# A fused two-layer program: routing and token transfers first at its head, another order of the feed-forward, scalings and last groups at its end

## The reference, cut to what matters

```python
# x: (8, 512, 128), two layers
xn = layernorm(x)
x = x + mamba(xn) + moe(xn)          # layer 0
xn = layernorm(x)
x = x + window_attention(xn) + swiglu(xn)   # layer 1
# mamba: proj = xn @ in_proj.T; conv over 4 steps, silu -> u; x_proj, three rmsnorms -> dt, B, C
#   h = exp(dt*A) * h + (dt*u) * B   (512 steps, 256 channels, 16 states);  y = sum(h * C) + u * D
#   out = (y * silu(gate)) @ out_proj.T
# moe: top_idx = argmax(xn @ gate_w.T + gate_b + expert_bias)  (8 experts)
#   out = w2[e] @ relu(w1[e] @ xn + b1[e]) + b2[e] for the token's expert e
# window_attention: 16 heads of 8, keys at most 32 positions away, softmax, then @ Wo + bo
# swiglu: (silu(xn @ wg.T) * (xn @ wu.T)) @ wd.T, hidden width 384, weights given as int32 / 127
```

## Time and profile before

| | us |
|---|---|
| median of 3 runs | 1018.65 (1018.41 to 1019.23) |
| the profiled execution | 1021.74 |
| its span | 1019.9 |
| busy: TensorE, VectorE, ScalarE, GpSimd | 810.4, 760.9, 638.1, 434.0 |

### The profile page before, as it was taken

How to read it: one execution, slowest core, us unless ns; L and a number is a source line. 1 busy time by engine, 2 the same in 40 slices (tenths; PEclk the granted TensorE clock), 3 DMA queues, 4 the chain that set the end, 5 groups by cost and what they waited for, 6 DMA issues and landing times.

```text
span 1019.9 us, 15614 instructions
## 1 busy us (share of the span) xinstructions
PE 810.4 (79%) x5226; PEld 560.0 (55%) x5226; DVE 760.9 (75%) x1059; ACT 638.1 (63%) x1976; POOL 434.0 (43%) x248
## 2 busy tenths in 40 slices
PE   1855788776788788988898799889888986899785
PEld 0622787664554565556555656565556554556443
DVE  7769443445867897789778977897888888786475
ACT  0233566644579566956795689568956884595554
POOL 2368331104564156516742573266426632571100
PEclk9957899998789888999999989999999998899898
DMA  6564799775434254235414541464145414550000
GB/s 218 172 193 137 233 280 299 225 203 132 119 79 98 60 143 99 64 103 145 115 46 120 149 99 41 119 152 106 32 123 148 106 41 124 129 122 15 19 11 12
DMA packets 85952, 123.20 MB, mean 121 GB/s; under 512 B 8560, under 2 KB 43760, under 8 KB 85744
## 3 DMA queue, kind: packets, MB, share of 16 engines
q1 hardware_dynamic: 79584, 115.38, 41.6%
q0 software_dynamic: 6288, 6.82, 3.0%
HBM read 106.21 MB, written 12.29 MB: 116 GB/s over the span
## 4 chain that ended last, share of the span: by engine, by line
PE 36%; DVE 24%; ACT 14%; issue 12%; POOL 8%; DMA 3%; SPq 1%; DVEq 0%; POOLq 0%; ACTq 0%
DVE hst L818 9%; PE more L1446 6%; ACT pexp L1118 5%; PE y_bank L1314 5%; DVE dBu L810 5%; POOL xs_d L1184 3%; ACT dA L1040 3%; POOL hc L1216 3%; ACT pT L1131 2%; PE work L1333 1%; PE work_l L1458 1%; PE work L1359 1%; PE work L1496 1%; PE work_l L1428 1%; PE work L1292 1%
## 5 line engine op out<-in xcount | busy, mean ns | idle before, releaser
L1216 POOL TENSOR_TENSOR hc<-hst,bcr 128x1024 f32<-128x1024 f32 x116 | 273.7, 2360 | 423.1 <-DVE dBu L810 401.6
L818 DVE TENSOR_TENSOR_SCAN hst<-dA,dBu 128x1024 f32<-128x1024 f32 x128 | 291.8, 2280 | 1.9 <-ACT dA L1040 0.9
L1040 ACT ACTIVATE dA<-dt,neg_a 128x511 f32<-128x511 f32 x256 | 171.0, 726 | 34.0 <-DVE hst L818 31.4
L810 DVE TENSOR_TENSOR dBu<-dtu,bcr 128x1024 f32<-128x1024 f32 x128 | 160.4, 1253 | 11.9 <-DMA bcr<-bc_d 1.5
L1314 PE MATMUL y_bank<-pk,hc 128*128 128x128 f32 x1024 | 153.9, 299 | 14.5 <-POOL hc L1216 10.9
L1314 PEld LDWEIGHTS y_bank<-pk,hc 128*128 128x128 f32 x1024 | 128.8, 154 | 50.8 <-issue 23.3
L1446 PE MATMUL more<-pk,pexp 128*96 128x128 f32 x480 | 109.4, 301 | 48.5 <-ACT pexp L1118 43.0
L1446 PEld LDWEIGHTS more<-pk,pexp 128*96 128x96 f32 x480 | 58.1, 129 | 95.4 <-issue 51.9
L1118 ACT ACTIVATE pexp<-work,nmax 128x96 f32<-128x96 f32 x240 | 77.9, 337 | 30.8 <-DVE nmax L965 30.7
L1131 ACT COPY pT<-more 96x512 f32<-96x512 f32 x120 | 69.9, 582 | 36.8 <-PE more L1446 36.3
L965 DVE TENSOR_REDUCE nmax<-work 128x4 f32<-128x384 f32 x60 | 33.4, 557 | 78.3 <-PE work L1367 57.5
(11 more groups left out here) (363 smaller groups left out, 1524.7 us busy)
## 6 DMA issues: line engine op xcount, KB each, us to landing
bcr<-bc_d SPq DMA_DIRECT2D x128, 512.0 KB, 5.1
qbd<-in_wx SPq DMA_DIRECT2D x8, 578.0 KB, 4.6
o_all<-in_wx SPq DMA_DIRECT2D x8, 578.0 KB, 4.8
pT<-in_wx SPq DMA_DIRECT2D x8, 578.0 KB, 5.1
kT<-in_wx SPq DMA_DIRECT2D x8, 578.0 KB, 5.1
vw<-in_wx SPq DMA_DIRECT2D x8, 578.0 KB, 5.0
xs_d<-rbuf POOLq DMA_DIRECT2D x1, 2560.0 KB, 9.7
hst<-in_hidden SPq DMA_DIRECT2D x8, 256.0 KB, 6.6
```

The costliest lines, as they stand in the source:

```text
L810: v.tensor_tensor(dBu[:], dtu[par], bcr[n % RING][:, 0:1, :].to_broadcast([P, NH, L]), ALU.mult).then_inc(s_dBu, 1)
L818: v.tensor_tensor_scan(hst[n % 2][:].rearrange("p h t -> p (h t)"), dA[n % 2][:].rearrange("p h t -> p (h t)"), dBu[:].rearrange("p h t -> ...
L1040: s.activation(dA[n % 2][:, h, 1:L], dt[par][:, h, 1:L], ACT.Exp, scale=neg_a[:, h, n:n + 1]).then_inc(s_dA, 1)
L1216: g_.tensor_tensor(hc[n % 2][:], hst[n % 2][:], bcr[n % RING][:, 1:2, :].to_broadcast([P, NH, L]), ALU.mult).then_inc(s_hc, 1)
```

## The change

At the head, `LEAD` now holds the statistics, normalisation, transposes and gates of all eight sequences, then four constants, `pick`, `count`, `place`, the other constants, and the scatters of sequences 0 to 2. Each engine walks through `LEAD` before turn -1. The scatters of sequence 3 stand in slot 8 of turn -1, the others in slot 9. The four first loads of x go ahead of the packed weights, the feed-forward weights come later. The zeros are written from a zeroed half of `dA[1]` and issued ahead of the last power on GpSimd. The wait for all constants moves from the start of TensorE, ScalarE and GpSimd to the units that use them. The expert stage begins in slot 3.

At the end, the feed-forward of sequence 6 leaves turn 7 for `LAST`, behind `y_end`, with banks of its own (5 to 7, which the preparation and `dBu` no longer need). The scaling goes from VectorE to GpSimd. The feed-forward of sequence 7 comes in slots 2 to 7 with its two halves a slot apart, and writes to `z[0]` and `dA`. The averages of sequence 6 move from slot 3 to 7 and its output from 4 to 8 and 9. The last groups are written out by hand.

```diff
-MOE_AT = 4
+MOE_AT = 3
...
+FFN_UNITS = ("fg", "fs", "fu", "fh", "rden")
...
 def last_turn():
     a, f = B - 1, B - 2
-    out = [("y_end", 0, a), ("rdT", 0, f), ("gated", 0, a), ("yT", 0, a)]
-    out += [(name, 0, a) for name in ("out", "x1", "ln_a", "ln_b", "q", "k", "v0", "v1")]
-    for t in range(G + 3):
-        if 1 <= t <= G:
+    out = [("y_end", 0, a), ("fg", 0, f), ("fu", 0, f), ("gated", 0, a), ("fs", 0, f), ("fh", 0, f), ("yT", 0, a),
+           ("fg", 1, f), ("out", 0, a), ("fu", 1, f), ("x1", 0, a), ("ln_a", 0, a), ("fs", 1, f), ("fh", 1, f),
+           ("fg", 2, f), ("fu", 2, f), ("ln_b", 0, a), ("fs", 2, f), ("fh", 2, f), ("rden", 0, f), ("rdT", 0, f)]
+    out += [(name, 0, a) for name in ("q", "k", "v0", "v1")]
+    for t in range(G):
+        if t >= 1:
             out.append(("exp", t - 1, a))
...
+    out += [(name, k, a) for name, k in (
+        ("exp", G - 1), ("scale", G - 2), ("turn", G - 2), ("values", G - 3), ("proj", 2), ("own", G - 4),
+        ("scale", G - 1), ("turn", G - 1), ("own", G - 3), ("values", G - 2), ("y_last", 2), ("own", G - 2),
+        ("values", G - 1), ("own", G - 1), ("proj", 3), ("y_last", 3))]
...
-LEAD = [("stats", 0), ("stats", 1), ("norm", 0), ("stats", 2), ("norm", 1)]
+def lead():
+    out = [("stats", 0)]
+    for k in range(B):
+        if k + 1 < B:
+            out.append(("stats", k + 1))
+        out += [("norm", k), ("xT", k)]
+        if k > 0:
+            out.append(("gate", k - 1))
+    out += [("gate", B - 1), ("route_consts", 0), ("pick", 0), ("count", 0), ("place", 0), ("consts", 0)]
+    return out + [("scatter", k) for k in range(3)]
...
-    put(-1, 14, ("scatter", 0))
+    put(-1, 8, ("scatter", 3))
+    put(-1, 9, *[("scatter", k) for k in range(4, B)])
...
                     v.reciprocal(rden[:, :, k], den[:, :, k]).then_inc(s_rden, 1)
-                    dve.wait_ge(s_rden, b + k + 1)
-                    v.tensor_tensor(pexp[k % 2][:], pexp[k % 2][:], rden[:, :, k:k + 1].to_broadcast([P, RG, KW]),
-                                    ALU.mult).then_inc(s_norm, 1)
...
+                    elif name == "scale":
+                        pool.wait_ge(s_rden, b + k + 1)
+                        g_.tensor_tensor(pexp[k % 2][:], pexp[k % 2][:], rden[:, :, k:k + 1].to_broadcast([P, RG, KW]),
+                                         ALU.mult).then_inc(s_norm, 1)
```

More of the change, by code:

```diff
@@ L229, in l1_bank @@
         return LAST_BANK[key]
+    if b == B - 2 and key in FFN_BANK:
+        return FFN_BANK[key]
     return L1_BANK[key]
@@ L802, in early @@
                             v.tensor_tensor(bias_rest[:], bias_rest[:], bias_part[:], ALU.subtract).then_inc(s_bias, 1)
+            for name, k in LEAD:
+                early(name, k)
             def times_b(n, b, par):
@@ L1032, in early @@
                     last.then_inc(s_mr, 1)
+            for name, k in LEAD:
+                early(name, k)
             def decays(n, b, par):
+                if b == 0 and n == 0:
+                    act.wait_ge(s_const, CONSTS)
+                if b == 0 and n == 1:
+                    act.wait_ge(s_zero, 16)
                 if n == 0:
```

175 lines of the change are left out of this document (92 added, 83 removed).

## The result

| | before | changed |
|---|---|---|
| median of the runs | 1018.62 us (4 runs, 1018.41 to 1019.23) | 1028.13 us (4 runs, 1027.01 to 1032.25) |
| ratio, 95% interval | | 1.0081 [1.0051, 1.0111] |
| profiled execution, span | 1021.74 us, 1019.9 us | 1027.95 us, 1026.2 us |

The forecast was 1010.5 us, faster; by the medians the kernel got 9.5 us slower.

The account below looks back on a forecast made before the run. Limits seen: first expert tile waiting for scattered tokens, the expert-tile loop, then a chain to the first scores and VectorE in the score groups. Head +1, way to scores -7.4, loop 0, last groups -1.7: 1010.5 us, range 1004 to 1018.

Parts of the forecast that it names:

- Head, routing: Start of program: eight norms end near 24, routing takes 9.4 us, slot table at 35.5 instead of 55.58 us.
- Head, what waits for it: First sequence's preparation, moved behind routing: convolution at 41.8, first scan step at 84.1 instead of 74.66 us.
- Head, the expert stage: First expert tile at about 105.5, where it was 105.0; head +1 us, between -4 and +12.
- The scan's start holds it: First expert tile waits behind sequence 1's second convolution matmuls, 15.1 us after the first scan step; nothing left of 20 us.
- rival (3): Head gives back the end's gain: first scan step near 90, first tile near 112, +7.5; 1017 us, no change; chance 0.10.
- Middle: Sequences 1 to 6: no engine's order changes, so the stretch is carried over at its present time.
- End, the way to the first scores: Last scan to first scores: y_end 4.3 us earlier, projections at full clock; -7.4 us, bounds -4 and -8.
- End, the score loop: Sixteen score groups: 6.5 us round three groups, 2.15 per group against 2.23; net 0, from -2.5 to +5.
- The last groups: Last exponential to last y: 7.6 to 9.2 us where it was 9.9; -1.7, between 0 and -2.3.
- The sum: Whole kernel: +1 - 7.4 + 0 - 1.7 = -8.1 us, giving 1010.5 us for the median.
- late head: The case of rival (3): late first scan step and first tile, head +7.5 us; 1017 us; chance 0.10.
- slow loop: Score loop slower: GpSimd handovers 0.2 us each, averages stop two groups, +4; 1014.5 us; chance 0.12.

Follow-up runs that it names:

- e5: The changed kernel with 14 wide matmuls on zeros ahead of everything on TensorE: 1029.50 us, ratio 1.0114 to the kernel before.
- e9: The changed kernel with the expert stage two slots earlier (MOE_AT = 1 instead of 3): 1031.51 us, ratio 1.0107 to the kernel before.
- e13: e12 with VectorE's first instruction held until the tenth of 32 wide matmuls, a plain delay at the start: 1020.61 us, ratio 1.0016.
- e16: The kernel of e13 run and profiled once more, nothing changed: 1020.36 us in one run.
- e2: The kernel before with the changed tail alone, head of before: 1019.73 us, ratio 0.9997.
- e3: As e2, with the scaling of the last sequence's groups back on VectorE: 1015.74 us, ratio 0.9967 to the kernel before.
- e4: The kernel before with only y_end ahead of sequence 6's feed-forward; loop and last groups of before: 1017.97 us, ratio 0.9981.
- e7: e4 with sequence 6's final sums at group 10 and sequence 7's feed-forward at groups 4, 6, 8: 1012.30 us, ratio 0.9945.
- e10: e7 with each part of sequence 7's feed-forward split over two groups, parts two groups earlier: 1016.33 us, ratio 0.9970.
- e11: e7 with the change's order of the last groups: 1011.47 us, ratio 0.9918 to the kernel before.
- e12: e11 with 22 wide matmuls on zeros on TensorE at the start: 1010.98 us, ratio 0.9918 to the kernel before.
- e15: The changed kernel measured and profiled again, nothing changed: 1028.86 us against 1020.21 for the kernel before, ratio 1.0097.
- e6: The kernel before with only the last sequence's scalings moved to GpSimd: 1023.05 us against 1019.89, ratio 1.0030.
- e14: Changed head with preparation before routing and ten wide matmuls on zeros ahead, with e11's tail: 1018.80 us, ratio 0.9967 to the kernel before.

## Why the prediction was wrong

**Head, routing: the step that failed first.** "Eight of them in one piece ... end near 24" and the 9.4 us of routing were right (23.16 + 1.11; 32.66 to 42.09). Between the two the prediction has no term for TensorE at all: it lets the routing begin at 26 us, when VectorE is done, as if the transposes and gates ended with the norms. They end at 32.6, because TensorE does them at 2.45 us a sequence, no faster than the norms come, and only from 12.52 on. In the head of before the same work ran behind wide convolutions at 0.60 + 0.96 us, and hid beside other work; at the start of the program it runs at the lower level. Slot table: 35.5 forecast, 42.1 measured. e5 shows this cause by itself: with TensorE warm the slot table is there 5.0 us earlier.

**Head, what waits for it.** The order of the chain was right and so were most durations: from slot table to first convolution 6.3 forecast, 7.3 measured; from there to the first scan step 42.3 forecast, 43.1 measured. One link was wrong: the scatters ahead of xdn were to set the time of the transposes behind it, but xdn was done at 73.86 and the transposes at 75.53 waited for VectorE's sg (74.78 + 0.69). That they came 26.3 us behind the first convolution, 25.5 forecast, is luck in that link. All 8.2 us by which the first scan step missed 84.1 came down from the routing, but for 1.8. But the forecast itself already moved that step by 9.4 us, and the prediction let all of it vanish behind the expert stage's start.

**Head, the expert stage.** "The scan's start holds it" was right: the second convolution matmuls of sequence 1 start 15.1 us behind the first scan step, as forecast, and the first tile starts behind them (107.45 + 5.32), not behind the scatters, the last of which ended at 94.4. The allowance for a scan step inside the stage was fair (129.6 against 128.4 us, e9 shows where it ends to be fair). With the first tile at 115 instead of 105.5 the head's term became +8.9 instead of +1. This is the sum's largest error, 7.9 us; rival (3) had that path (a late first scan step takes the first tile with it), with +7.5, but from other causes (both convolutions at 6.31 us, slow scatters, late loads), and came to "no change" with an end of -9. The head's own range reached to +12, so the measured +8.9 lies inside it.

**Middle.** Taken at its present time; it lost 2.2 us in the means. The stretch takes 692.6 and 694.3 us in the changed kernel's two profiles and 689.3 to 695.1 in the eight with the head of before, so the loss is not clear of their spread. The two long turns of the changed kernel, 3.4 us together, are seen in both; no order changed there, and e13 and e16 exclude the mere shift, so their cause stays open.

**End, the way to the first scores.** Right in size and cause: -7.4 forecast, -7.6 measured; out projection 2.02 us, q and k 1.98, at full clock. With the head of before, q and k took 3.78 us in seven of nine profiles with this order (e2, e3, e4, e7, e10, e11, e16; 3.23 in e12, 1.98 in e13), and only 5.65 us were had, near the 5.8 that the prediction gave for a fallen clock. The full 7.6 of the changed kernel is thus in part luck. The Trainium skill (TensorE: Matmul & The Clock Gate, section HAM oscillation) has idle gaps bring the clock down and a filled stream keep it. The stream was not wholly filled here, and the rule does not tell the two cases apart: before q and k TensorE idled 1.25, 0.31 and 0.3 us in the changed kernel as in e4, which has the same order up to there, and q and k took 1.98 us at a granted clock of 1.00 in the one, 3.78 at 0.57 to 0.58 in the other.

**End, the score loop: the second step that failed.** Forecast 0, measured +5.5 us in the mean: +4.7 in e15 with TensorE at the full level, +6.3 in the first profile. The way round was counted as 6.5 us over three groups with feed-forward parts "about 2.2 us per part as before". It left out where the parts stand. TensorE's two matmuls (1.7 us) lie between a group's turn and the next scores, so on the way round; before, VectorE did the part's two products meanwhile, and in the change it has them one group later and idles. e10 measures this at 1.7 us of waiting over three parts, and as much again where TensorE's clock falls behind the longer idle time. The scaling on GpSimd took 0.83 us, less than the 1.01 forecast, and is the largest piece all the same: with it each of seven rounds of the changed order is 0.3 us longer in e15 than in e3, 2.2 us together. The remaining 0.7 us of the 4.7 lie between e3, without its stretch at the lower level, and e10, whose sums of sequence 6 stand two groups later. So the way round, with the parts on it, was longer than VectorE's work, and the 0.56 us freed there bought nothing. In the order of before (e6) the loop itself did not suffer from the scaling, as forecast, but from the averages ahead of it in GpSimd's queue; the prediction had that wait as a term, 1.2 us at group 7, and in the changed kernel it is nothing: the averages run from 980.70 to 983.63, in GpSimd's idle time before the scaling at 986.04. The Trainium skill's rule (GPSIMD Engine Reference, section Engine selection) pointed that way, by another price: it has two-input elementwise work about twice as slow on GpSimd, and 0.83 against 0.56 is 1.5 times.

**The last groups.** Forecast -1.7, measured -1.3 in the change, and -2.0 where the scaling is on VectorE (e11 against e7's and before's end).

**The sum.** +1 - 7.4 + 0 - 1.7 became +8.9 + 2.2 - 7.6 + 5.5 - 1.3 = +7.7. The head and the loop each came out inside or just at the end of the range that the prediction gave them (up to +12 and +5); the range of the whole, up to 1018, allowed only 7.5 us above the forecast and so left out that both go wrong. The chances have the same fault: head and loop were each given a chance of going wrong with the other right, and cases in which both do (late head 0.10, slow loop 0.12) had none of their own.

The version to take is e11 (1011.5 us, 0.8% below before; e7 and e12 are not to be told from it): the head of before, y_end ahead of sequence 6's feed-forward, its final sums at group 10, scaling on VectorE, the change's order of the last groups.

## What to carry to other kernels

A duration belongs to the state of its engine: before small matmuls are moved to the start of a program, look whether the stretch from which their price is read was warmed by wide ones. When a loop is bound by one engine, draw the way round it with everything that stands on it in every queue: taking work off the bounding engine gains only until that way is as long, and filler between two links of it is free only while the bounding engine has work for that time; and look what stands in the queue that receives the work. Before a difference is put down to an edit, look whether both profiles ran at the same clock level in that stretch. And an earlier start of a stage is no gain where the work in front of it merely moves inside; follow the last instruction of the stage, not its first.

## What the runs showed of the hardware

- The granted clock of the windows reads 1.00 from 10 to 30 us of the changed kernel, while the durations there are those of the lower level (1.09 us for four transposes); in e5, where wide matmuls ran before, the windows read 1.00 as well and the same four take 0.60. In these profiles durations tell the level at the start of the program, the clock column does not:

```profile
10.00:20.00 10.00, 7.49 (x36) 7.25 (x36) 9.69 (x59) 2.39 (x5) 4.35 (x5) 1.00 0.88 261
20.00:30.00 10.00, 10.00 (x51) 10.00 (x50) 5.59 (x25) 2.58 (x5) 2.86 (x3) 1.00 0.99 345
```

- TensorE did not come up to the full level over the 20 us from 12.52 to 32.62, busy all the time with transposes and 8-column products. After wide matmuls (e5) the same work ran at it until about 25 us; in e14, with ten wide ones that ended at 12.0, only until 18.3.
- GpSimd's product of 128x384 took 0.83 us in all sixteen cases in the score loop; the xdn product of that shape took 1.00 to 1.02 before. Beside eight of the sixteen VectorE was at work on PSUM, and these took no longer than the others. The scatters of before did stretch: the four that took 1.83 to 1.96 us ran beside VectorE's products `dBu`, `hc` and `u`, those wholly beside a scan took 0.95 to 0.96.
